# A four-layer graph network: the third layer's per-destination sums as running sums along partitions, with transfers issued from SyncE

## The chip, the cores and the metric

The kernel runs on one core of one Trainium2 chip. The metric is the device time of one execution in microseconds, the median of several runs; lower is better. PE is the matrix engine, DVE is VectorE, ACT is ScalarE, POOL is GpSimd, SP is SyncE.

## What is computed

A graph of 6250 nodes with 64 features and 200000 edges, sorted by destination, goes through four layers, each `x = x + layer(relu(layernorm(x)))`. The first is an attention over edges, the second four rounds of neighbour sums, the fourth two hops of a normalised neighbour sum. The third is the one changed:

```
features = H[src]
Y = relu(concatenate([features, Xe], axis=1) @ M_W.T + M_b)
Z = segment_sum(Y, dst, num_segments=6250)
H_next = relu(concatenate([H, Z], axis=1) @ U_W.T + U_b)
```

`Xe` is 200000 x 64, so each edge has a message of 64 numbers, and `Z` sums the messages of the edges with the same destination.

## The kernel before

Nodes are padded to 49 tiles of 128 (6272), edges to 1568 chunks of 128 (200704). The stages run one after the other, with a barrier between them: attention loop over the edges and its combination (first layer, which also counts a dense matrix A of edge counts), second layer on A with matrix products, then `last_layers`: a table `H @ M_h.T + b` written to DRAM (`tab_l`), the edge loop `sum_chunks` (L1003), the update `update_pieces` (L1206), and the two hops of the fourth layer on the transposed matrix AT.

`sum_chunks` works on groups of 8 chunks, 196 in all; four groups make a block, of which there are 49, and two groups a half block. The loop is written once and repeated by hardware loops; `steps` gives its order to every engine. The order on each engine is the order of the code:

- POOL gathers the rows of `tab_l` for the sources of a group, 8 indirect DMAs of 128 rows (L1193), once the index list `ixs` is there and the buffer `gl` has been read.
- PE multiplies the edge features `ea` by the weights (L1100), then transposes half a row block of A (49 products with the identity per block, L1110), which has nothing to do with the messages and is done here for the fourth layer, then does the sums (L1118). An fp32 product shows as two matmul records.
- DVE compares, for a whole group, the destinations of the chunk's 128 edges along the free dimension (`dall`, a list broadcast to all partitions) with the destination of the edge in each partition (`dst`), which gives `S` (128 x 8 x 128, L1082); then it adds the product and the gathered rows (`t1`, L1088).
- ACT evicts the transposes (L1148), stores the block of AT, does the ReLU (`msg`, L1160), issues the loads of index list, destination list and features for the group two half blocks later (L1135, L1137, L1140), and evicts and stores the sums (L1169, L1171).

In this layout an edge's number within its chunk is its partition. `S` times `msg` gives, in the row of every edge, the sum over all edges of its chunk with the same destination. The update gathers for each node the row of its last edge (`last_row`) and adds a carry for nodes whose edges begin in an earlier chunk: the last rows of the 1568 chunks are loaded, transposed in 14 pieces, summed by a scan of 1568 columns, transposed back and scattered to DRAM by 14 indirect DMAs (L1466), and the carry rows `U` are loaded again (L1258) and multiplied by a mask (L1335). After this, 7 pieces of 7 node tiles are summed (L1340, L1342), multiplied by the weights, normalised and split for the hops.

Of the kernel before, what the change touches and what calls it, by code (L numbers as in the profile page):

```python
# [293 lines left out]
def carry_rows(nc, g, step, dump, node, a, b):  # L294
# [4 lines left out]
    e = [g.next_c[:, k, :] for k in range(4)]  # L299
# [11 lines left out]
    step(v.tensor_copy(g.carry_to[:, :], node[:, :]))  # L311
# [70 lines left out]
def segment_ends(nc, g, top):  # L382

    g.last_row = top.sb("last_row", [P, NT], I32)
    g.last_f = top.sb("last_f", [P, NT])
    g.has = top.sb("has", [P, NT])
# [5 lines left out]
    with Stage(nc, "ends") as st:  # L392
# [86 lines left out]
        with st.block() as block:  # L479
# [6 lines left out]
            def _(dve):  # L486
# [14 lines left out]
                step(v.tensor_tensor(g.con[:, :], tmp[:, :], g.has[:, :], ALU.mult))  # L501
                step(v.tensor_tensor(tmp[:, :], cl[:, :], z[:, :], ALU.subtract))
# [11 lines left out]
                carry_rows(nc, g, step, dump, node, ca, cb)  # L514
# [488 lines left out]
def sum_chunks(nc, g, name, wb):  # L1003
# [3 lines left out]
    with Stage(nc, name) as st:  # L1007
# [4 lines left out]
        halves = (range(0, (NK + 1) // 2), range((NK + 1) // 2, NK))  # L1012
        dst_i = st.sb("dst_i", [P, NCH], I32)
        dst = st.sb("dst", [P, NCH])
# [3 lines left out]
        dall = [st.sb(f"dall{s}", [P, G, P], I32) for s in range(RB)]  # L1018
        ea = [st.sb(f"ea{s}", [D, G * P]) for s in range(RB)]
        S = [st.sb(f"S{s}", [P, G, P]) for s in range(RB)]  # L1020
# [3 lines left out]
        o = [st.sb(f"o{s}", [P, G, D]) for s in range(RB)]  # L1024
        a = [st.sb(f"a{s}", [P, NP], BF16) for s in range(R)]
        at = [st.sb(f"at{s}", [P, NT, P], BF16) for s in range(R)]
        pb = [st.ps(f"pb{s}", [P, G, D]) for s in range(R)]
        pm = [st.ps(f"pm{s}", [P, G, D]) for s in range(R)]
        pt = [st.ps(f"pt{k}", [P, 512]) for k in range(TB)]
        s_c, s_k, s_one, s_go, s_tp, s_tv = (st.sem(k) for k in ("c", "k", "one", "go", "tp", "tv"))  # L1030
        s_msg, s_mm, s_ev, s_a, s_st, s_mb, s_t1 = (
            [st.sem(f"{k}{s}") for s in range(R)] for k in ("msg", "mm", "ev", "a", "st", "mb", "t1"))
        s_da, s_S, s_out, s_ea, s_ix = ([st.sem(f"{k}{s}") for s in range(RB)] for k in ("da", "S", "out", "ea", "ix"))
# [4 lines left out]

        def wait_earlier(eng, sem, u):

            if not (isinstance(u, int) and u < 2):
                eng.wait_ge(sem, u - 1)
        Arows = g.A[0:NP * HI, :].rearrange("(n h) l -> n (h l)", h=HI)
        with st.block() as block:

            @block.sync
            def _(sp):
                sp.dma_start(dst_i[:, :], g.d["dst_cols"]).then_inc(s_c, 16)
                sp.dma_start(wbs[:, :], wb).then_inc(s_c, 16)
                sp.wait_ge(s_c, 32)  # L1050
                sp.sem_inc(s_k, 1)

            @block.vector
            def _(dve):
                nc.vector.tensor_copy(eye[:, :], g.ident[:, :]).then_inc(s_one, 1)
                dve.wait_ge(s_k, 1)
                nc.vector.tensor_copy(dst[:, :], dst_i[:, :]).then_inc(s_one, 1)
# [14 lines left out]
        with st.block() as block:  # L1072

            @block.vector
            def _(dve):
                def body(u, dt, b, n, h):
                    for s in range(R):
                        c0 = u * (R * G) + s * G
                        q = h * R + s
                        wait_earlier(dve, s_mm[s], u)  # L1080
                        dve.wait_ge(s_da[q], dt * 16 + 16)
# [4 lines left out]
                        dve.wait_ge(s_mb[s], u + 1)  # L1086
                        dve.wait_ge(s_gl[q], dt * (16 * G) + 16 * G)
                        nc.vector.tensor_tensor(t1[q][:, :, :], pb[s][:, :, :], gl[q][:, :, :], ALU.add)\  # L1088
                            .then_inc(s_t1[s], 1)

                steps(dve, body)

            @block.tensor
            def _(pe):
                def body(u, dt, b, n, h):
                    for s in range(R):
                        wait_reuse(pe, s_t1[s], u)
                        pe.wait_ge(s_ea[h * R + s], dt * 16 + 16)
                        for j in range(G):
                            mm = nc.tensor.matmul(pb[s][:, j, :], ea[h * R + s][:, j * P:(j + 1) * P], wbs[:, :],  # L1100
                                                  start=True, stop=True)
                        mm.then_inc(s_mb[s], 1)
                    if h == 0:
                        pe.wait_ge(s_a[b], n * 16 + 16)
                    for k in halves[h]:
                        before = k - TB if k >= TB else max(j for j in range(NK) if j % TB == k % TB) - NK
                        if before >= 0 or not (isinstance(dt, int) and dt == 0):
                            pe.wait_ge(s_tv, dt * NK + (before + 1))
                        for m, q in enumerate(blocks[k]):
                            mm = nc.tensor.matmul(pt[k % TB][:, m * P:(m + 1) * P], a[b][:, q * P:(q + 1) * P],  # L1110
                                                  eye[:, :], start=True, stop=True)
                        mm.then_inc(s_tp, 1)
                    for s in range(R):
                        wait_reuse(pe, s_ev[s], u)
                        pe.wait_ge(s_S[h * R + s], dt + 1)
                        pe.wait_ge(s_msg[s], u + 1)
# [3 lines left out]
                        mm.then_inc(s_mm[s], 1)  # L1120
# [4 lines left out]
            def _(act):  # L1125
                def load_block(dt, b):
                    if not known(dt, 2):
                        act.wait_ge(s_tp, dt * NK + (-NK))
                    act.dma_start(a[b][:, :], Arows[bass.ds(dt * P, P), :]).then_inc(s_a[b], 16)

                def load_group(u, dt, h, s):
                    c0 = u * (R * G) + s * G
                    q = h * R + s
                    wait_reuse(act, s_gl[q], dt * (16 * G))
                    act.dma_start(ixs[q][:, :], g.d["src_cols"][:, bass.ds(c0, G)]).then_inc(s_ix[q], 16)  # L1135
                    wait_reuse(act, s_S[q], dt)
                    act.dma_start(dall[q][:, :, :].rearrange("p g e -> p (g e)"),  # L1137
                                  g.d["dst"][bass.ds(c0 * P, G * P)].partition_broadcast(P)).then_inc(s_da[q], 16)
                    wait_earlier(act, s_mb[s], u)
                    act.dma_start(ea[q][:, :], g.d["ea64T"][:, bass.ds(c0 * P, G * P)]).then_inc(s_ea[q], 16)  # L1140

                def body(u, dt, b, n, h):
                    if h == 0:
                        wait_reuse(act, s_st[b], n * 16)
# [1154 lines left out]
```

## Time and profile before

| | us |
|---|---|
| timed runs, median of 3 | 6479.86 (6473.62 to 6487.33) |
| profiled execution, span from first to last instruction | 8670.1 |
| attention loop | 448.6 to 4102 |
| second layer and table | 4102 to 5105.9 |
| set-up and loop of `sum_chunks` | 5105.9 to 8087.5 |
| `update_pieces` | 8087.5 to 8255.8 |
| two hops | 8255.8 to 8670.1 |

The profiled execution is 2190 us longer than the timed runs; no other time of it is given. A row of a timeline has the start, the duration, the engine, the line of the kernel, the operation with its output and inputs, and in brackets the idle time before it with what ended it. A releaser called "issue" means that the engine waited for nothing that the profile shows. For a gather, the duration is GpSimd's work of issuing it, and not the landing of the data.

### The profile page before, as it was taken

The numbers are of one execution on the slowest core, as the hardware profiler recorded it, in microseconds if no ns is written. First come the engines' busy times: TensorE is split into PE (matmuls) and PEld (weight loads), VectorE is DVE, ScalarE is ACT, GpSimd is POOL, SyncE is SP. The second block draws the span as 40 slices with busy tenths as digits, with TensorE's granted clock in tenths as the row PEclk, the third lists the DMA queues.
The fourth block names the chain that finished last, engine by engine and source line by source line (L and its number), as shares of the span: only waits on it lengthen the run. The fifth ranks groups of instructions, "written<-read, shape, count | busy, mean of one in ns | idle before, by whom it ended". The sixth has DMA issues, their size and how long they took to land. (4 is left out here: it accounts for less than half of the span.)

```text
span 8670.1 us, 115438 instructions
## 1 busy us (share of the span) xinstructions
PE 5309.3 (61%) x35178; PEld 4390.0 (51%) x35178; DVE 2969.1 (34%) x3937; ACT 1847.1 (21%) x3914; POOL 3549.7 (41%) x3427
## 2 busy tenths in 40 slices
PE   2256556566666556667199955555565555656599
PEld 2234344444444434445089955555455554545499
DVE  6545544555544554445532121111111111111321
ACT  0023333333333333334000001112111111211200
POOL 5554353344444334344300025454554545555400
PEclk9567776776766776667589965555555555555599
DMA  8133333333333333333289934444444444444298
GB/s 304 38 96 97 105 98 91 97 107 95 110 95 94 96 102 95 92 96 105 65 288 365 365 117 138 144 131 152 124 150 140 136 146 129 153 132 144 78 375 337
DMA packets 659238, 1262.19 MB, mean 146 GB/s; under 512 B 167977, under 2 KB 467562, under 8 KB 633364
## 3 DMA queue, kind: packets, MB, share of 16 engines
q10 hardware_dynamic: 254028, 651.47, 23.4%
q1 hardware_dynamic: 295624, 491.69, 15.8%
q0 software_dynamic: 109184, 115.05, 6.1%
q14 instruction: 319, 2.61, 0.1%
q8 instruction: 83, 1.36, 0.1%
HBM read 924.66 MB, written 490.51 MB: 163 GB/s over the span
## 5 line engine op out<-in xcount | busy, mean ns | idle before, releaser
L697 POOL DMA_INDIRECT att_gl<-tab_l,att_ix x1568 | 1617.2, 1031 | 2013.0 <-DVE att_msg L850 1468.4
L1193 POOL DMA_INDIRECT sum_gl<-tab_l,sum_ixs x1568 | 1552.8, 990 | 1445.2 <-DMA sum_ixs<-in_src_cols 920.4
L938 ACT ACTIVATE att_acc<-att_pc 128x392 bf16<-128x392 f32 x2352 | 1085.4, 496 | 2271.2 <-remote 1131.8
L716 PE MATMUL att_pc<-att_acc,att_ohv 128*128 128x392 bf16 x2352 | 901.0, 383 | 989.7 <-ACT att_acc L938 523.4
L1088 DVE TENSOR_TENSOR sum_t<-sum_pb,sum_gl 128x512 f32<-128x512 f32 x196 | 135.3, 690 | 2596.8 <-remote 1890.2
L713 PE MATMUL att_pc<-att_ohl,att_ohv 128*128 128x392 bf16 x2352 | 904.0, 384 | 145.0 <-DVE att_ohl L813 84.5
L716 PEld LDWEIGHTS att_pc<-att_acc,att_ohv 128*128 128x128 bf16 x2352 | 248.2, 106 | 1435.5 <-ACT att_acc L938 787.1
L1110 PE MATMUL sum_pt<-sum_eye,sum_a 128*128 128x128 bf16 x2401 | 361.5, 301 | 869.6 <-issue 786.9
L1118 PE MATMUL sum_pm<-sum_msg,sum_S 128*128 128x64 f32 x3136 | 651.5, 403 | 260.6 <-ACT sum_msg L1160 258.7
L1100 PE MATMUL sum_pb<-sum_wbs,sum_ea 64*128 64x64 f32 x3136 | 704.7, 415 | 149.8 <-issue 122.3
L754 PE MATMUL att_pm<-att_msg,att_S 128*128 128x69 f32 x3136 | 618.4, 357 | 289.8 <-issue 145.2
L1118 PEld LDWEIGHTS sum_pm<-sum_msg,sum_S 128*128 128x128 f32 x3136 | 633.3, 313 | 282.1 <-ACT sum_msg L1160 230.6
L1100 PEld LDWEIGHTS sum_pb<-sum_wbs,sum_ea 64*128 64x128 f32 x3136 | 684.0, 327 | 149.5 <-issue 110.6
L1110 PEld LDWEIGHTS sum_pt<-sum_eye,sum_a 128*128 128x128 bf16 x2401 | 242.8, 136 | 994.3 <-issue 870.2
L732 PEld LDWEIGHTS att_pl<-att_xe,att_S 128*128 128x128 f32 x3136 | 643.8, 231 | 162.5 <-issue 142.7
L754 PEld LDWEIGHTS att_pm<-att_msg,att_S 128*128 128x128 f32 x3136 | 572.5, 271 | 299.5 <-issue 294.7
L1148 ACT ACTIVATE sum_at<-sum_pt 128x512 bf16<-128x512 f32 (+1 forms) x637 | 307.4, 591 | 1544.3 <-remote 672.4
L801 DVE TENSOR_TENSOR att_S<-att_dall,att_dst 128x896 f32<-128x896 int32 x224 | 245.0, 1094 | 1109.6 <-remote 926.3
L1932 PE MATMUL l_pn<-l_E,l_a 128*128 128x192 bf16 x7203 | 603.2, 246 | 12.0 <-DVE l_E L1803 12.0
L1932 PEld LDWEIGHTS l_pn<-l_E,l_a 128*128 128x128 bf16 x7203 | 595.5, 98 | 14.1 <-issue 12.2
L732 PE MATMUL att_pl<-att_xe,att_S 128*128 128x64 f32 x3136 | 582.0, 288 | 0.0
L813 DVE TENSOR_TENSOR att_ohl<-att_c_lo,cnt_lo 128x2352 bf16<-128x2352 f16 x448 | 547.3, 1222 | 0.0
(373 smaller groups left out, 5241.2 us busy)
## 6 DMA issues: line engine op xcount, KB each, us to landing
A<-att_acc SPq DMA_DIRECT2D x2352, 98.0 KB
l_a<-A SPq DMA_DIRECT2D x147, 1568.0 KB, 9.1
att_dall<-in_dst ACTq DMA_DIRECT2D x224, 448.0 KB
sum_dall<-in_dst ACTq DMA_DIRECT2D x196, 512.0 KB
hop_at<-AT SPq DMA_DIRECT2D x56, 1568.0 KB, 8.8
sum_a<-A ACTq DMA_DIRECT2D x49, 1568.0 KB, 9.5
AT<-sum_at ACTq DMA_DIRECT2D x49, 1568.0 KB, 6.3
l_at<-AT SPq DMA_DIRECT2D x42, 1568.0 KB, 8.8
```

Source lines behind the costliest of these rows:

```text
L697: nc.gpsimd.indirect_dma_start(out=gl[s][:, c, :], out_offset=None, in_=g.tab_l, in_offset=bass.IndirectOffsetOnAxis(ap=ix[s][:, c:c + 1], ...
L713: nc.tensor.matmul(pc[c][m % 2][:, 0:LO], ohv[c][h][:, m, :, 0], ohl[c][h][:, m // 2, :, m % 2], start=True, stop=False)
L716: nc.tensor.matmul(pc[c][m % 2][:, 0:LO], ohv[c][h][:, m, :, 1], acc[c][(at0[t] + m - 1) % CR][:, :], start=False, stop=True).then_inc(s_m ...
L732: mm = nc.tensor.matmul(pl[k % 2][:, j * D:(j + 1) * D], S[t // NQ][:, k * GQ + j, :], xe[k][:, j, :], start=False, stop=j == GQ - 1, skip ...
L754: mm = nc.tensor.matmul(pm[:, j * W0:(j + 1) * W0], S[s][:, q * GQ + j, :], msg[:, q * GQ + j, :], start=True, stop=True)
L813: v.tensor_tensor(ohl[c][h][:, 0:w // 2, :, :], spread(c_lo2[:, :, :].unsqueeze(1), [P, w // 2, LO, 2]), spread(g.lo[:, bass.ds(n0, w)].re ...
L938: nc.scalar.activation(acc[c][n % CR][:, :], pc[c][m % 2][:, 0:LO], ACT.Copy).then_inc(s_acc[c], 1)
L1100: mm = nc.tensor.matmul(pb[s][:, j, :], ea[h * R + s][:, j * P:(j + 1) * P], wbs[:, :], start=True, stop=True)
L1110: mm = nc.tensor.matmul(pt[k % TB][:, m * P:(m + 1) * P], a[b][:, q * P:(q + 1) * P], eye[:, :], start=True, stop=True)
L1118: mm = nc.tensor.matmul(pm[s][:, j, :], S[h * R + s][:, j, :], msg[h * R + s][:, j, :], start=True, stop=True)
L1193: nc.gpsimd.indirect_dma_start(out=gl[q][:, j, :], out_offset=None, in_=g.tab_l, in_offset=bass.IndirectOffsetOnAxis(ap=ixs[q][:, j:j + 1] ...
L1932: mm = nc.tensor.matmul(pn[k][q // 2][:, q % 2 * 3 * D:(q % 2 + 1) * 3 * D], a[c][:, t, q * P:(q + 1) * P], E3[p % 2][:, c * PIECE + t, :] ...
```

## The change

Edges are laid out along partitions: partition p has the edges p x 1568 to p x 1568 + 1567, and chunk c is column c of all of them. Consecutive edges of one destination then lie in the same partition in consecutive chunks, and the sum within a destination is a running sum from chunk to chunk: `run[c] = run[c-1] * same[c] + msg[c]`, where `same` says whether an edge has the destination of the one before. This takes one scalar_tensor_tensor per chunk on DVE, each waiting for the one before by a semaphore, and delayed by one group against the add. The comparison `S`, the destination lists, the sums on PE, their evictions and the buffers for them go. PE's transposes are dealt out in quarters behind the products of the four groups, and the products have four PSUM buffers (two before). All loads and stores of the loop are issued by SP, which has nothing to issue there before. Carries are now between 128 partitions and not between 1568 chunks: one transpose each way, a scan of 128 columns, one scatter, and no mask.

```diff
-        dst = st.sb("dst", [P, NCH])
+        same = st.sb("same", [P, NCH])
...
+                v.tensor_tensor(same[:, 1:NCH], dst_i[:, 1:NCH], dst_i[:, 0:NCH - 1], ALU.is_equal).then_inc(s_one, 1)
+                step(v.tensor_copy(next_f[:, :, 0], next_i[:, :]))
+                dve.wait_ge(s_io, 1)
+                step(v.tensor_copy(dump[:, :], dump_i[:, :]))
+                carry_rows(nc, g, step, [next_f[:, k, :] for k in range(4)], dump, node, ca, cb, g.carry_p)
...
+                def add(dt, q):
+                    wait_reuse(dve, s_msg[q], dt)
+                    dve.wait_ge(s_mb[q], dt + 1)
+                    dve.wait_ge(s_gl[q], dt * (16 * G) + 16 * G)
+                    v.tensor_tensor(t1[q][:, :, :], pb[q][:, :, :], gl[q][:, :, :], ALU.add).then_inc(s_t1[q], 1)
+
+                def sums(dt, q):
+                    c0 = dt * (RB * G) + q * G
+                    wait_reuse(dve, s_out[q], dt * 16)
+                    dve.wait_ge(s_msg[q], dt + 1)
+                    for j in range(G):
+                        before = run[q][:, j - 1, :] if j else run[(q - 1) % RB][:, G - 1, :]
+                        if not known(c0 + j, 1):
+                            dve.wait_ge(s_run, c0 + j)
+                        v.scalar_tensor_tensor(out=run[q][:, j, :], in0=before, scalar=same[:, bass.ds(c0 + j, 1)],
+                                               in1=msg[q][:, j, :], op0=ALU.mult, op1=ALU.add).then_inc(s_run, 1)
...
-                        nc.vector.tensor_tensor(
-                            S[q][:, :, :], dall[q][:, :, :],
-                            spread(dst[:, bass.ds(c0, G)].unsqueeze(2), [P, G, P]), ALU.is_equal)\
-                            .then_inc(s_S[q], 1)
...
-                        for j in range(G):
-                            mm = nc.tensor.matmul(pm[s][:, j, :], S[h * R + s][:, j, :], msg[h * R + s][:, j, :],
-                                                  start=True, stop=True)
...
+                def load_group(dt, q):
+                    c0 = dt * (RB * G) + q * G
+                    wait_reuse(sp, s_gl[q], dt * (16 * G))
+                    sp.dma_start(ixs[q][:, :], g.d["src_rows_p"][:, bass.ds(c0, G)]).then_inc(s_ix[q], 16)
+                    wait_reuse(sp, s_mb[q], dt)
+                    sp.dma_start(ea[q][:, :], g.d["ea64P"][:, bass.ds(c0 * P, G * P)]).then_inc(s_ea[q], 16)
+
+                def keep(dt, q):
+                    sp.wait_ge(s_run, dt * (RB * G) + (q * G + G))
+                    sp.dma_start(tot_rows(g, dt * (RB * G) + q * G), run[q][:, :, :]).then_inc(s_out[q], 16)
...
+                        if not (isinstance(dt, int) and dt + 1 >= NT):
+                            load_group(dt + 1, q)
+                        if q:
+                            keep(dt, q - 1)
+                        elif not known(dt, 1):
+                            keep(dt - 1, RB - 1)
...
-                step(vec.tensor_tensor(U[:, :, :], U[:, :, :], spread(g.con[:, :].unsqueeze(2), [P, NT, W]), ALU.mult))
...
-                for b in range(B):
-                    nc.gpsimd.indirect_dma_start(
-                        out=carries, in_=crow[:, b, :], in_offset=None,
-                        out_offset=bass.IndirectOffsetOnAxis(ap=g.carry_to[:, b:b + 1], axis=0)).then_inc(s_sc, 16)
+                nc.gpsimd.indirect_dma_start(
+                    out=carries, in_=crow[:, :], in_offset=None,
+                    out_offset=bass.IndirectOffsetOnAxis(ap=g.carry_p[:, 0:1], axis=0)).then_inc(s_sc, 16)
```

VectorE in the body of the loop, before: a comparison and an add per group (two groups shown; ISA and REGISTER_ALU are waits and sums on registers).

```order
L1081 ISA
L1082 ISA
L1082 TENSOR_TENSOR sum_S<-sum_dall,sum_dst 128x1024
L1086 REGISTER_ALU
L1087 ISA
L1088 TENSOR_TENSOR sum_t<-sum_pb,sum_gl 128x512
L1082 ISA
L1082 TENSOR_TENSOR sum_S<-sum_dall,sum_dst 128x1024
L1088 TENSOR_TENSOR sum_t<-sum_pb,sum_gl 128x512
```

The same place after the change: the end of one chain, the add, and the beginning of the next chain.

```order
L1108 SCALAR_TENSOR_TENSOR sum_run<-sum_run,sum_same,sum_msg 128x64
L1098 TENSOR_TENSOR sum_t<-sum_pb,sum_gl 128x512
L86 REGISTER_ALU
L1107 REGISTER_ALU
L1108 ISA
L1108 SCALAR_TENSOR_TENSOR sum_run<-sum_run,sum_same,sum_msg 128x64
L1107 REGISTER_ALU
L1108 ISA
L1108 SCALAR_TENSOR_TENSOR sum_run<-sum_run,sum_same,sum_msg 128x64
```

The comparison is gone, and eight dependent steps, each with a register sum and a register wait in front, follow each add.

GpSimd in the update stage, before (`upd_J` are the rows of the nodes' last edges, `car` the carries in DRAM):

```order
L1458 DMA upd_J<-tot,top_last_row 128x64 x14
L1466 DMA car<-upd_crow,top_carry_to 7840x64 x14
L1458 DMA upd_J<-tot,top_last_row 128x64 x35
```

and after:

```order
L1476 DMA upd_J<-tot,top_last_edge 128x64 x14
L1483 DMA car<-upd_crow,top_carry_p 7840x64
L1476 DMA upd_J<-tot,top_last_edge 128x64 x35
```

Thirteen of the 14 scatters between the gathers are gone.

## Rows read from the trace of the kernel before

**Rows 1.** The page of the profile, its span.
```profile
span 8670.1 us, 115438 instructions
```

**Rows 2.** Stretches: length, busy us (records) by engine, granted clock, DMA share, GB/s.
```profile
core 0: us, PE busy (x) PEld busy (x) DVE busy (x) ACT busy (x) POOL busy (x), PEclk, DMA share, GB/s
...
448.60:4102.00 3653.40, 2264.13 (x11515) 1541.46 (x11515) 1857.90 (x2511) 1253.08 (x2791) 1617.15 (x1568) 0.70 0.34 99
...
5119.30:8067.60 2948.30, 1694.55 (x8612) 1549.11 (x8612) 352.47 (x389) 536.53 (x1019) 1552.76 (x1568) 0.51 0.46 139
8067.60:8087.50 19.90, 11.47 (x63) 10.93 (x62) 2.52 (x3) 5.08 (x11) 0.00 (x0) 0.50 0.42 112
8087.50:8255.80 168.30, 75.49 (x322) 63.44 (x322) 61.00 (x124) 35.07 (x72) 65.70 (x63) 0.50 0.21 58
```

**Rows 3.** The page's groups: out<-in, count | busy us, mean ns | idle before, releaser.
```profile
L697 POOL DMA_INDIRECT att_gl<-tab_l,att_ix x1568 | 1617.2, 1031 | 2013.0 <-DVE att_msg L850 1468.4
L1193 POOL DMA_INDIRECT sum_gl<-tab_l,sum_ixs x1568 | 1552.8, 990 | 1445.2 <-DMA sum_ixs<-in_src_cols 920.4
```

**Rows 4.** Gathers of both loops: count, ns min/median/max, first and last start; a wait.
```profile
L697 POOL DMA_INDIRECT att_gl<-tab_l,att_ix x1568: 939/945/1870, 448.6 to 4068.3; - x196
...
L1193 POOL DMA_INDIRECT sum_gl<-tab_l,sum_ixs x1568: 938/945/1962, 5119.3 to 8066.6; - x196
...
  DMA sum_ixs<-in_src_cols: 920.4, 58
```

**Rows 5.** Timeline of PE, quick stretch: start us, us, line, what, count.
```profile
6533.61 7.09 PE L1100 MATMUL sum_pb<-sum_wbs,sum_ea 64*128 64x64 f32 x32
...
6545.37 5.75 PE L1118 MATMUL sum_pm<-sum_msg,sum_S 128*128 128x64 f32 x32 [1.67 <-ACT sum_msg L1160]
6551.05 1.33 PE L1100 MATMUL sum_pb<-sum_wbs,sum_ea 64*128 64x64 f32 x5
```

**Rows 6.** The same columns as in the stretches: a slow and a quick one.
```profile
6499.80:6517.00 17.20, 2.55 (x10) 1.40 (x9) 0.00 (x0) 0.60 (x1) 13.18 (x14) 0.50 0.16 42
6533.60:6551.10 17.50, 15.83 (x94) 15.41 (x93) 3.65 (x4) 5.87 (x11) 11.89 (x11) 0.60 0.78 227
```

**Rows 7.** Timeline: gathers beside VectorE's add and comparison in the changed loop.
```profile
6537.17 0.94 POOL L1193 DMA_INDIRECT sum_gl<-tab_l,sum_ixs  x1 [0.30 <-issue]
6537.42 0.69 DVE L1088 TENSOR_TENSOR sum_t<-sum_pb,sum_gl 128x512 f32<-128x512 f32 x1 [12.13 <-PE sum_pb L1100]
6538.03 1.22 DVE L1082 TENSOR_TENSOR sum_S<-sum_dall,sum_dst 128x1024 f32<-128x1024 int32 x1
6538.42 1.65 POOL L1193 DMA_INDIRECT sum_gl<-tab_l,sum_ixs  x1 [0.30 <-issue]
```

**Rows 8.** Timeline of the update stage, GpSimd, SyncE and VectorE.
```profile
8088.16 0.94 POOL L1458 DMA_INDIRECT upd_J<-tot,top_last_row  x1 [20.62 <-POOLq L101]
...
8108.34 0.95 POOL L1466 DMA_INDIRECT car<-upd_crow,top_carry_to  x1 [0.30 <-issue]
...
8126.71 0.77 SPq L1258 DMA_DIRECT2D l_y<-car  x1
...
8137.83 3.42 DVE L1335 TENSOR_TENSOR l_y<-l_y,top_con 128x3136 f32<-128x3136 f32 x1 [30.30 <-DMA l_y<-car]
8138.24 3.83 POOL L1458 DMA_INDIRECT upd_J<-tot,top_last_row  x1 [0.30 <-issue]
8141.29 0.62 DVE L1340 TENSOR_TENSOR upd_J<-upd_J,top_has 128x448 f32<-128x448 f32 x1
```

**Rows 9.** Timeline of the end of the changed loop.
```profile
8072.38 0.69 DVE L1088 TENSOR_TENSOR sum_t<-sum_pb,sum_gl 128x512 f32<-128x512 f32 x1 [1.10 <-DMA sum_gl<-tab_l,sum_ixs]
...
8081.99 0.34 ACTq L1171 DMA_DIRECT2D tot<-sum_o  x1
```

**Rows 10.** Groups of VectorE by shape, 5119 to 8255 us: count | busy us, mean ns.
```profile
L1352 DVE SCALAR_TENSOR_TENSOR upd_xm<-upd_mean,top_x 128x448 f32<-128x448 f32 x7 | 4.4, 624 | 0.2
...
L1360 DVE TENSOR_TENSOR upd_v<-upd_v,upd_deg 128x7 f32<-128x7 f32 x7 | 1.2, 166 | 0.2
```

More of the change, by code:

```diff
@@ L291, in node_table, with carry_rows @@
             after(nc, g, st, res)
-def carry_rows(nc, g, step, dump, node, a, b):
+def carry_rows(nc, g, step, e, dump, node, a, b, to):
     v = nc.vector
-    e = [g.next_c[:, k, :] for k in range(4)]
     step(v.tensor_copy(node[:, :], e[0]))
@@ L310, in carry_rows @@
     step(v.tensor_tensor(node[:, :], node[:, :], dump[:, :], ALU.add))
-    step(v.tensor_copy(g.carry_to[:, :], node[:, :]))
+    step(v.tensor_copy(to[:, :], node[:, :]))
 class Degrees:
@@ L501, in _ @@
                 step(v.tensor_tensor(g.con[:, :], tmp[:, :], g.has[:, :], ALU.mult))
+                step(v.scalar_tensor_tensor(out=tmp[:, :], in0=cl[:, :], scalar=float(P), in1=cnt[:, :],
+                                            op0=ALU.mult, op1=ALU.add))
+                step(v.tensor_scalar(tmp[:, :], tmp[:, :], -1.0, 0.0, ALU.add, ALU.max))
+                step(v.tensor_scalar(tmp[:, :], tmp[:, :], float(EP - 1), None, ALU.min))
+                step(v.tensor_copy(g.last_edge[:, :], tmp[:, :]))
                 step(v.tensor_tensor(tmp[:, :], cl[:, :], z[:, :], ALU.subtract))
@@ L513, in _ @@
                 step(v.tensor_copy(dump[:, :], dump_i[:, :]))
-                carry_rows(nc, g, step, dump, node, ca, cb)
+                carry_rows(nc, g, step, [g.next_c[:, k, :] for k in range(4)], dump, node, ca, cb, g.carry_to)
 def expand_rows(nc, g, st, res):
@@ L1101, in body @@
                                                   start=True, stop=True)
[L1102 to L1116, printed above, removed]
[L1117 to L1120 removed]
+                        mm.then_inc(s_mb[q], 1)
@@ new lines, in body @@
+                        if q == 0:
+                            pe.wait_ge(s_a[b], n * 16 + 16)
+                        for k in quarters[q]:
+                            before = k - TB if k >= TB else max(j for j in range(NK) if j % TB == k % TB) - NK
+                            if before >= 0 or not known(dt, 1):
+                                pe.wait_ge(s_tv, dt * NK + (before + 1))
+                            for m, r in enumerate(blocks[k]):
+                                mm = nc.tensor.matmul(pt[k % TB][:, m * P:(m + 1) * P], a[b][:, r * P:(r + 1) * P],
+                                                      eye[:, :], start=True, stop=True)
+                            mm.then_inc(s_tp, 1)
@@ L1125, in _, with body @@
             def _(act):
+                def body(u, dt, b, n, h):
+                    for s in range(R):
+                        q = h * R + s
+                        if q == 0:
+                            wait_reuse(act, s_st[b], n * 16)
+                        for k in quarters[q]:
+                            r = blocks[k]
+                            act.wait_ge(s_tp, dt * NK + (k + 1))
+                            nc.scalar.activation(at[b][:, r[0]:r[-1] + 1, :],
+                                                 pt[k % TB][:, 0:len(r) * P].rearrange("p (m e) -> p m e", e=P), ACT.Copy)\
+                                .then_inc(s_tv, 1)
+                        if not known(dt, 1):
+                            act.wait_ge(s_run, dt * (RB * G) + (q * G + G - RB * G))
+                        act.wait_ge(s_t1[q], dt + 1)
+                        nc.scalar.activation(msg[q][:, :, :], t1[q][:, :, :], ACT.Relu).then_inc(s_msg[q], 1)
@@ L1126, in load_block, with _ @@
+                steps(act, body)
+            @block.sync
+            def _(sp):
                 def load_block(dt, b):
                     if not known(dt, 2):
[L1128 to L1140, printed above, removed]
@@ L1142, in body @@
[L1142 to L1150 removed]
+                        sp.wait_ge(s_tp, dt * NK + (-NK))
@@ L2251, in lay_out @@
     a["dst_next"] = nxt.reshape(4, CQ, CP).transpose(2, 0, 1)
+    a["src_rows_p"] = src.reshape(P, NCH)
+    a["dst_rows_p"] = dst.reshape(P, NCH)
+    a["last_p"] = dst[NCH - 1::NCH]
+    a["last_p_prev"] = np.concatenate([np.full(1, -1, np.int32), dst[NCH - 1::NCH][:-1]])
+    beyond = np.concatenate([dst, np.full(2 * NCH, NP, np.int32)])
+    a["next_p"] = np.stack([beyond[np.arange(1, P + 1) * NCH + k] for k in (-1, 0, NCH - 1, NCH)], 1)
     rows = np.full((NCH + 1, P + 2), NP + 1, np.int32)
```

161 lines of the change are left out of this document (72 added, 89 removed).

## The prediction

> **What bounds the kernel now.** I read the stages first, then the engine that sets the pace of the changed one. The profiled execution spans 8670.1 us, the timed runs have a median of 6479.9: 2190.2 us less, so before anything is summed it must be settled which waits of the trace are not in the time. The change touches the edge loop of the third layer (2948.3 us of the span) and the two short stages behind it; the attention loop of the first layer takes 3653.4 [rows 1, 2].
>
> Both loops issue 1568 indirect gathers on GpSimd. One lasts 945 ns in the median, and undisturbed ones follow each other every 1.25 us [rows 3, 4, 7]. That is a floor of 1568 x 1.25 = 1960 us for each loop, whatever the other engines do. In the third layer's loop the 2948 us are this floor, plus 1552.8 - 1568 x 0.945 = 71 us by which gathers last longer, plus some 917 us in which GpSimd waits; the view of the gathers names 920.4 us in 58 waits, for the index load [rows 3, 4]. ScalarE issues that load behind its ReLU, in order behind its evictions of PE's transposes, so the wait goes back to PE.
>
> And PE has two speeds there that the work doesn't explain. In one stretch of 17.2 us it leaves 10 matmul records and is busy 2.55 us; in another of 17.5 it leaves 94, at about the same granted clock (0.50, 0.60) [rows 6]. In the quick stretch a whole half block (two groups' products, 28 transposes, two groups' sums) goes from 6533.61 to 6551.05, 17.4 us, with 16 gathers (20.0 us) to be fed by it [rows 5]. At that speed PE never holds GpSimd up; only the slow stretch does, once in each of the 49 blocks. The time says that much of this is not in the timed runs: the attention loop has its own floor of 1960 of 3619.7 us between its first and last gather [rows 4], so it can give back 1660 at most, and the changed loop must give at least 530 of the 2190. Timed, it lasts between 1960 and 2418 us. I take the case in which GpSimd's waits are gone there. Then GpSimd is active all the time and not for 2031 of 2948 us, and the 71 us of long gathers grow to 71 x 2948 / 2031 = 103. **Timed loop before: 2063 us.**
>
> **Part by part.** *The comparison and the sums on PE go.* 196 comparisons (1.22 us on VectorE), the loads that feed them, 1568 fp32 products and 196 evictions go. With GpSimd as the bound, none of this counts on PE or ScalarE. What counts is what the comparison does to a gather: the one that begins at 6538.42, 0.39 us into a comparison, takes 1.65 us, while one beside the add, which has an operand in PSUM, takes 0.94 [rows 7]. So all 103 us are put down to comparisons (0.53 us each), and go. This is where a page speaks otherwise. The Trainium skill ("SBUF — State Buffer", section "Who interferes with whom") says that a tensor_tensor with two SBUF inputs takes only the shared read interface, which descriptor generation is inferred not to need. By that rule neither comparison nor new sum would lengthen a gather, and this term would be 0. The trace disagrees with 1.65 against 0.94 us, and I go by the trace.
>
> *1568 running sums come.* Each is a scalar_tensor_tensor over 128x64 with two SBUF inputs, the same kind that holds a gather up, only shorter. Nearest rows: 166 ns for 7 elements, 624 ns for 448 [rows 10], so 1.04 ns an element and 0.225 us for 64. Eight in each 10 us of gathers are 18% of the time. A gather that meets one waits for what is left of it, 0.11 us on average: 1568 x 0.18 x 0.11 = 32 us. Lower bound 0, upper bound under the rivals. That VectorE lets a gather through between two of its instructions, I read from 8138.24: this gather ends at 8142.07, 0.82 us after the end of L1335 (8141.25), although L1340 began 0.04 us later [rows 8]. **Loop: 1960 + 32 = 1992, 71 us less.**
>
> *The chain on VectorE* doesn't bind. A step waits for the one before, and has a register instruction and a register wait in front: 0.225 us plus at least the 0.04 between two instructions in rows 8, at a guess 0.35. With the add of 0.69 a group needs 3.5 of its 10 us. It would bind from (10 - 0.7) / 8 = 1.16 us a step.
>
> *SyncE issues.* Per group now index load, feature load, store; per block a write of the transposed block and a load. In front of each index load it waits for the store before, which waits for the running sums. Behind that wait are queued the next index and feature loads. The index load for group q of the next block is issued when the gather of group q has landed, three groups (30 us) before GpSimd needs it, and a running sum is 3 us late at most, so nobody waits. ScalarE loses its issue work and 196 evictions: nothing, it isn't the bound. The destination lists (196 x 128x1024 int32, 100 MB) that no longer move were beside the gathers: 0, or a gain in landing, which no one waits for but at the end.
>
> *Beginning and end of the loop.* The set-up gets a comparison over 1567 columns in place of a cast, 13 dependent tiny operations and 4 more in an earlier stage: 17 x 0.17 [rows 10] and their waits, +5 us, in the open. At the end 9.6 us pass from the last add to the last store (8072.38 to 8081.99) [rows 9], through ReLU, product and eviction; now add 0.7, ReLU, and two groups of 8 steps, 6.4: -3 us.
>
> *Update stage.* 14 scatters of carries become one. The first piece's sums begin at 8141.29, behind the multiplication of the carry rows (8137.83, 3.42 us) and their load, issued at 8126.71, after the 14 scatters from 8108.34 on. Now: 14 gathers from 8088.16 at 1.25 us, one scatter at about 8106, its landing, load issued near 8108, the same 11.1 us to land, no multiplication: near 8119 [rows 8]. -22 us. The pieces behind are a chain over PE, ScalarE and VectorE that keeps its spacing, and the row gathers (35 x 1.25 = 44 us from 8107 on) stay ahead of it, so all of the 22 should reach the end. The two hops behind it start earlier by that and stay as they are.
>
> **Sum:** -71 + 5 - 3 - 22 = -91. Against the median: 6479.9 - 91 = **6389 us**. The span of the profiled execution falls by more, as the 917 us of waits hang on PE, which loses a third of the block's work and the step between add and index load: 8670 - 91 - up to 917, so down to 7660.
>
> **Rivals.**
> *PE's slow stretches are partly in the timed runs.* Then the timed loop before lasts up to 2418, and the change takes away up to 426 instead of 71: between 6389 and 6034. For: rows 6 show nothing that PE waits for, so they can't exclude a real cause. Against: the attention loop has 1524 us of waits of its own, enough for most of the 2190. Shared in proportion, with the longer gathers counted, 46 us would be left in this loop: 6343.
> *The long gathers don't change*, because they aren't in the time or the short operations cost as much as the long ones: only +5 - 3 - 22 is left, 6460. In this case the gathers would lie where the page of the Trainium skill named above puts them.
> *Slower: a gather can't get in between chained sums.* If it has to wait for the end of a chain of 8 (2.8 us), one gather in each group waits some 2.2 us: 196 x 2.2 = 431 instead of 103, so 6479.9 + 328 - 20 = 6788. It decides from 0.63 us a group ((103 + 20) / 196). Against it stands 8138.24 in rows 8; for it, that this is one case, with a 3.4 us operation.
> *Slower: a step of the chain takes over 1.16 us.* At 1.4 a group takes 11.9 us and the loop 2333: 6730. Against: the gaps of 0.04 in rows 8; for: register waits between the steps, which no row shows.
>
> **How the numbers follow.** Forecast (6330 to 6445) 0.55; PE rival 0.15; no change of long gathers 0.15; blocked by the chain 0.10; slow steps 0.05. The two slower cases, 0.15, lie above; of the PE rival I leave out what is below 6200, about 0.05. Range 6200 to 6480. A measurement of this kernel can tell about 0.2% (13 us) from no change. The no-change case lies 20 us below the median and falls on either side of that line, half each. Faster 0.55 + 0.15 + 0.08 = 0.78; same 0.07; slower 0.15.
>
> **What would show it.** In the trace after: gathers of the loop at 1.25 us with few above 1.1 us, and their busy sum near 1482 + 32 = 1514 instead of 1552.8; running sums of 0.2 to 0.25 us, under 4 us a chain; first piece's sums some 32 us after the update stage begins, not 54; GpSimd's waits for the index load far below 920. Wrong if the busy sum of the gathers rises, if GpSimd waits for the add, or if the median moves by much more than the loop's floor allows.

## The result

The changed kernel takes 6384.8 us (median; 6383.0 to 6396.1), the kernel before 6479.5: ratio 0.9857, 95% interval 0.9843 to 0.9871. The forecast was 6389. Its profiled execution spans 6384.6 us, so this trace is a trace of the timed kernel, which that of before (8670.1, [rows 1]) was not. A second profile of the unchanged kernel before came out at 6476.3 us; the comparison below uses that one in place of [rows 1 to 4]. Two timed executions, one of the kernel before (13610.9 us) and one of the run with twice the products (6945.5), had a lower mean granted clock (0.303 and 0.599, against some 0.73 in the others) and are left out of all ratios.

First the page of the changed kernel, its span and the group of the gathers:

```profile
span 6384.6 us, 112327 instructions
...
L1221 POOL DMA_INDIRECT sum_gl<-tab_l,sum_ixs x1568 | 1483.9, 946 | 495.5 <-issue 477.7
```

Then the views of the gathers and of the running sums (count: ns min/median/max, first and last start):

```profile
L1221 POOL DMA_INDIRECT sum_gl<-tab_l,sum_ixs x1568: 942/947/1007, 3866.9 to 5827.5; - x196
...
L1108 DVE SCALAR_TENSOR_TENSOR sum_run<-sum_run,sum_same,sum_msg x1568: 274/283/350, 3888.8 to 5835.6; 128x64 f32<-128x64 f32 x196
```

The loop lasts 1960.6 us from first to last gather, which is the floor of 1568 x 1.25. No gather takes longer than 1.007 us (before: up to 1.962, [rows 4]), GpSimd waits for nothing but itself ("issue" is the 0.30 us between gathers), and the 1568 running sums cost at most 2 us of gathers (1483.9 against 1568 x 0.945). One group of them on the timeline:

```profile
4805.26 0.95 POOL L1221 DMA_INDIRECT sum_gl<-tab_l,sum_ixs  x1 [0.30 <-issue]
4805.26 3.20 DVE L1108 SCALAR_TENSOR_TENSOR sum_run<-sum_run,sum_same,sum_msg 128x64 f32<-128x64 f32 x8
...
4806.51 0.95 POOL L1221 DMA_INDIRECT sum_gl<-tab_l,sum_ixs  x1 [0.30 <-issue]
...
4807.76 0.94 POOL L1221 DMA_INDIRECT sum_gl<-tab_l,sum_ixs  x1 [0.30 <-issue]
```

Three gathers begin inside the chain of eight and keep their 0.95 us. The chain takes 3.20 us, about 0.4 a step.

The loop as a stretch of the changed kernel (columns as in [rows 2]):

```profile
3866.80:5828.50 1961.70, 1010.67 (x5537) 907.24 (x5537) 558.76 (x1747) 417.72 (x832) 1483.88 (x1568) 0.50 0.49 157
```

PE is at 52% busy in the loop, at a granted clock of 0.50 (1.2 GHz), and DVE at 28%.

### The profile page after: what moved, and what is told of

Its sections match the earlier page's. It is cut to its first block and busy times, and to the rows that moved or that the text cites. A ratio compares the mean times of both kernels' runs of the same rounds, so it can differ in the third digit from the quotient of the medians.

```text
span 6384.6 us, 112327 instructions
## 1 busy us (share of the span) xinstructions
PE 4411.9 (69%) x32016; PEld 3631.9 (57%) x32016; DVE 3174.4 (50%) x5301; ACT 1726.3 (27%) x3718; POOL 3776.5 (59%) x3415
## 5 line engine op out<-in xcount | busy, mean ns | idle before, releaser
L703 POOL DMA_INDIRECT att_gl<-tab_l,att_ix x1568 | 1930.2, 1231 | 487.4 <-issue 470.5
L1221 POOL DMA_INDIRECT sum_gl<-tab_l,sum_ixs x1568 | 1483.9, 946 | 495.5 <-issue 477.7
L1141 PE MATMUL sum_pt<-sum_eye,sum_a 128*128 128x128 bf16 x2401 | 309.7, 310 | 932.2 <-ACT sum_at L1157 892.7
L722 PE MATMUL att_pc<-att_acc,att_ohv 128*128 128x392 bf16 x2352 | 863.0, 367 | 114.2 <-ACT att_acc L944 110.4
L738 PEld LDWEIGHTS att_pl<-att_xe,att_S 128*128 128x128 f32 x3136 | 605.1, 218 | 162.4 <-issue 140.8
L760 PE MATMUL att_pm<-att_msg,att_S 128*128 128x69 f32 x3136 | 560.0, 333 | 4.6 <-ACT att_o L933 2.7
L1163 ACT ACTIVATE sum_msg<-sum_t 128x512 f32<-128x512 f32 x196 | 123.7, 631 | 1541.6 <-DVE sum_t L1098 1463.9
L1108 DVE SCALAR_TENSOR_TENSOR sum_run<-sum_run,sum_same,sum_msg 128x64 f32<-128x64 f32 x1568 | 444.7, 284 | 172.4 <-DVE sum_run L1108 5.5
L760 PEld LDWEIGHTS att_pm<-att_msg,att_S 128*128 128x128 f32 x3136 | 518.7, 248 | 9.3 <-ACT att_o L933 3.5
L719 PEld LDWEIGHTS att_pc<-att_ohl,att_ohv 128*128 128x128 bf16 x2352 | 312.9, 133 | 368.4 <-DVE att_ohl L819 303.6
```

What stands on the lines that cost most here:

```text
L703: nc.gpsimd.indirect_dma_start(out=gl[s][:, c, :], out_offset=None, in_=g.tab_l, in_offset=bass.IndirectOffsetOnAxis(ap=ix[s][:, c:c + 1], ...
L719: nc.tensor.matmul(pc[c][m % 2][:, 0:LO], ohv[c][h][:, m, :, 0], ohl[c][h][:, m // 2, :, m % 2], start=True, stop=False)
L722: nc.tensor.matmul(pc[c][m % 2][:, 0:LO], ohv[c][h][:, m, :, 1], acc[c][(at0[t] + m - 1) % CR][:, :], start=False, stop=True).then_inc(s_m ...
L738: mm = nc.tensor.matmul(pl[k % 2][:, j * D:(j + 1) * D], S[t // NQ][:, k * GQ + j, :], xe[k][:, j, :], start=False, stop=j == GQ - 1, skip ...
L760: mm = nc.tensor.matmul(pm[:, j * W0:(j + 1) * W0], S[s][:, q * GQ + j, :], msg[:, q * GQ + j, :], start=True, stop=True)
L1108: v.scalar_tensor_tensor(out=run[q][:, j, :], in0=before, scalar=same[:, bass.ds(c0 + j, 1)], in1=msg[q][:, j, :], op0=ALU.mult, op1=ALU.a ...
```

## The experiments

All ratios are to the kernel before, measured on the same chip.

### The kernel before, once more

No edit. 

> The kernel before, unchanged, for a second profile. Theory (GpSimd sets the pace of the third layer's edge loop, comparisons lengthen its gathers, PE's slow stretches are not in the time): 6480 us; if this profile spans about 6480, its loop takes 2050 to 2070 us from first to last gather, the gathers' busy sum is near 1482 + 100 = 1585 us, and GpSimd's waits for the index load are near zero. Rival (PE's slow stretches are partly in the time): the same time, but the busy sum stays near 1553 and some 50 us or more of waits for the index load are left.

6473.9 us (ratio 1.000, 0.999 to 1.001). The span, and the group of the gathers in the view of GpSimd's groups, which also names the wait for the index load:

```profile
span 6476.3 us, 115438 instructions
...
L1193 POOL DMA_INDIRECT sum_gl<-tab_l,sum_ixs x1568 | 1556.4, 993 | 524.7 <-issue 477.2 <-DMA sum_ixs<-in_src_cols 47.4
```

and the view of the gathers:

```profile
L1193 POOL DMA_INDIRECT sum_gl<-tab_l,sum_ixs x1568: 941/947/1996, 3857.0 to 5890.3; - x196
```

The 920 us of waits for the index load in [rows 4] are gone; of the 47.4 left, none lies inside the loop (no two of its gathers start more than 2.3 us apart). The loop lasts 2033.3 us: 1959 of pitches and 74 by which gathers are longer (1556.4 - 1568 x 0.945), where 100 were expected. PE's slow stretches are neither in this execution nor, by their times near 6475 us, in the timed ones that are compared.

The same trace shows how a comparison holds a gather up:

```profile
4909.42 0.95 POOL L1193 DMA_INDIRECT sum_gl<-tab_l,sum_ixs  x1 [0.30 <-issue]
4910.02 1.22 DVE L1082 TENSOR_TENSOR sum_S<-sum_dall,sum_dst 128x1024 f32<-128x1024 int32 x1
4910.67 1.39 POOL L1193 DMA_INDIRECT sum_gl<-tab_l,sum_ixs  x1 [0.31 <-issue]
```

The gather of 4909.42 has begun 0.60 us before the comparison and isn't touched. The one of 4910.67 ends at 4912.06, 0.82 us after the comparison's end (4911.24). 167 of the 1568 gathers last longer than 1 us, on average 0.44 us more than the 0.945 of an undisturbed one.

Counted over the whole loop, this is a rule. 182 gathers begin inside a comparison that has more than 0.125 us left. All those for which the comparison had begun at least 0.04 us earlier end 0.81 to 0.83 us after it (the few with hardly more than 0.125 us left show no difference); the three that begin within 0.03 us of its start aren't touched. Since 0.945 - 0.82 is 0.125, a held gather waits for what the comparison has left beyond 0.125 us. All of the 74 us are in such gathers (73.3).

### A comparison put back into the changed kernel

```diff
                 def add(dt, q):
...
+                    v.tensor_tensor(junk[:, :, :], dst_i[:, 0:G * P].rearrange("p (g e) -> p g e", e=P),
+                                    spread(same[:, 0:G].unsqueeze(2), [P, G, P]), ALU.is_equal).then_inc(s_junk, 1)
                     v.tensor_tensor(t1[q][:, :, :], pb[q][:, :, :], gl[q][:, :, :], ALU.add).then_inc(s_t1[q], 1)
```

> The changed kernel with one comparison per group put back on VectorE, of the same size (128x1024, two operands in SBUF), whose output nobody reads. Theory (such an instruction holds up the gather that meets it): 196 x 0.53 to 0.6 us, 104 to 118 us more than 6385, so 6489 to 6503, gathers' busy sum near 1590. Rival (a comparison doesn't delay gathers, the gain came from elsewhere): 6385 to 6387.

6422.6 us (0.9898 to 0.9931): 38 us more than the changed kernel and than the next one, measured beside it, about a third of what was expected, and outside the rival too. The view of the gathers:

```profile
L1226 POOL DMA_INDIRECT sum_gl<-tab_l,sum_ixs x1568: 942/947/1977, 3867.5 to 5860.0; - x196
```

and the timeline around one comparison:

```profile
4805.36 0.94 POOL L1226 DMA_INDIRECT sum_gl<-tab_l,sum_ixs  x1 [0.30 <-issue]
4805.51 1.23 DVE L1101 TENSOR_TENSOR sum_junk<-sum_dst_i,sum_same 128x1024 f32<-128x1024 int32 x1 [5.07 <-DMA sum_gl<-tab_l,sum_ixs]
4806.61 0.95 POOL L1226 DMA_INDIRECT sum_gl<-tab_l,sum_ixs  x1 [0.30 <-issue]
```

Here the comparison begins 0.15 us behind a gather's start and ends 0.13 behind the next one's, and neither is longer. In this kernel it follows the landing of a gather directly, and most comparisons fall in this place (125 of 196 begin within 0.2 us behind a gather's start); 104 gathers begin inside a comparison with more than 0.125 us left, where before it were 182, and only 66 last over 1 us (167 before). An operation of 1.2 us can fit between two gathers, so its cost depends on where in the 1.25 us it begins, and 196 of them cost between 32 us (the loop is 1992.5 long) and the 74 of before. My expectation had taken 0.53 us each from the first trace.

### The same comparison with one operand from PSUM

```diff
-                                    spread(same[:, 0:G].unsqueeze(2), [P, G, P]), ALU.is_equal).then_inc(s_junk, 1)
+                                    spread(pb[q][:, :, 0:1], [P, G, P]), ALU.is_equal).then_inc(s_junk, 1)
```

> As the one before, but the comparison's second operand comes from PSUM: same number of elements, same place, output read by nobody. Theory (it is the second operand in SBUF that holds a gather up, not the load on VectorE): 6385 to 6387, busy sum 1484. Rival (any long instruction on VectorE, or its delay of the add, costs): as much as with both in SBUF, about 6490.

6384.5 us (0.9846 to 0.9879), the changed kernel's time. The page's groups of the gathers and of the added comparison:

```profile
L1226 POOL DMA_INDIRECT sum_gl<-tab_l,sum_ixs x1568 | 1481.1, 945 | 495.3 <-issue 477.6
...
L1101 DVE TENSOR_TENSOR sum_junk<-sum_dst_i,sum_pb 128x1024 f32<-128x1024 int32 x196 | 239.4, 1221 | 1023.3 <-DMA sum_gl<-tab_l,sum_ixs 1022.9
```

196 operations of 1221 ns, as long as the comparisons, and not a microsecond of gathers. 138 gathers begin inside one with more than 0.125 us left, and none is held. It is the second SBUF operand that holds them up; neither the length alone nor the later add does. The Trainium skill ("SBUF — State Buffer", "Who interferes with whom") says that a VectorE instruction with at most one SBUF input, outside the 2-port modes, doesn't contend with GpSimd: with that, this trace agrees. That tensor_tensor with two SBUF inputs leaves descriptor generation alone, which the same section infers, does not hold for these gathers. They take their index list from SBUF, and by the section's own rule that an instruction with two SBUF inputs contends with a GpSimd instruction that reads SBUF, they could be held; the prediction left that rule out.

### The kernel before with a narrow comparison

```diff
-                            S[q][:, :, :], dall[q][:, :, :],
-                            spread(dst[:, bass.ds(c0, G)].unsqueeze(2), [P, G, P]), ALU.is_equal)\
+                            S[q][:, :, 0:8], dall[q][:, :, 0:8],
+                            spread(dst[:, bass.ds(c0, G)].unsqueeze(2), [P, G, 8]), ALU.is_equal)\
```

> The kernel before with the comparison 8 columns wide in place of 128, so that most of S stays zero and the sums are left out; all loads, products and evictions stay. Theory: the held-up gathers go, 103 us less, about 6377, with all of PE's work still there. Rival (PE's work of the sums is what the change saved): 6480, no change.

6401.8 us (0.9867 to 0.9900): 70 us less than before, where 103 were expected. The view of the gathers:

```profile
L1195 POOL DMA_INDIRECT sum_gl<-tab_l,sum_ixs x1568: 940/944/990, 3861.8 to 5818.0; - x196
```

All of PE's products for the sums, their evictions and the loads of the destination lists are still there, and no gather is longer than 0.990 us. The loop lasts 1956.2 us, 77 less than before, and begins 5 us later. So the comparison's width alone carries the loop's whole gain, and neither PE's share of the work (1619 us busy in this loop, 1625 before) nor the 100 MB of lists carries any of it.

### Twice the products on PE

```diff
-                        for j in range(G):
+                        for j in [*range(G), *range(G)]:
                             mm = nc.tensor.matmul(pb[q][:, j, :], ea[q][:, j * P:(j + 1) * P], wbs[:, :],
```

> The changed kernel with every product of edge features and weights done twice into the same place: 1568 fp32 products more on PE, some 14 us in each block of 40, as much as the sums that the change takes from PE. Theory (GpSimd's 1.25 us per gather is the pace, PE hides behind it): the time of the changed kernel, ratio to before 0.985 to 0.987. Rival (PE's work counts): up to 49 x 14 us more, anything from 0.99 up.

6383.9 us (0.9839 to 0.9876), no change. With as much on PE as before the change (1665.9 us busy in the loop, 1625.0 before), the loop is at its floor: gathers from 3862.5 to 5823.7 us, 1961.2. The rival of PE falls.

### The update stage's part alone

```diff
-                for b in range(B):
+                for b in range(1):
                     nc.gpsimd.indirect_dma_start(
                         out=carries, in_=crow[:, b, :], in_offset=None,
...
-                step(vec.tensor_tensor(U[:, :, :], U[:, :, :], spread(g.con[:, :].unsqueeze(2), [P, NT, W]), ALU.mult))
```

> The kernel before with 1 scatter of carries in place of 14 and without the mask on the carry rows (so most carries and the mask are left out); loop and transposes as they were. Theory: 13 x 1.24 + 3.4 = 19.6 us less, of the 22 that the first piece's sums begin earlier in the changed kernel; ratio 0.9970. Rival (the pieces behind wait for something else and the gain of the stage's beginning is lost): 0.9985 to 1.

6455.2 us, ratio 0.9978 (0.9968 to 0.9988): 8 to 21 us less, with the expected 20 at the edge; the time alone would hardly tell it from the rival. The traces do: the stage begins at 5905.4 and its first sums at 5939.7, 34.3 us; in the second profile of before 5910.2 and 5964.0, 53.7. That is 19.4 us, and from there to the first product of the hops it is 99.0 us and 98.9, so nothing of it is lost there.

### Transfers issued from ScalarE

```diff
                         nc.scalar.activation(msg[q][:, :, :], t1[q][:, :, :], ACT.Relu).then_inc(s_msg[q], 1)
+                        if not (isinstance(dt, int) and dt + 1 >= NT):
+                            load_group(dt + 1, q)
+                        if q:
+                            keep(dt, q - 1)
+                        elif not known(dt, 1):
+                            keep(dt - 1, RB - 1)
```

> The changed kernel with all transfers of the loop issued from ScalarE in place of SyncE, behind each group's ReLU. Theory (the issuing queue is worth nothing, since index loads are three groups early): ratio to before 0.985 to 0.987. Rival (ScalarE's evictions wait behind the wait for the running sums, and with them PE's transposes and the index load): slower than the changed kernel by 1% or more.

6379.5 us (0.9843 to 0.9877). The queue that issues is worth nothing here, as costed.

### A second chain

```diff
+                        v.scalar_tensor_tensor(out=junk[q][:, j, :], in0=t1[q][:, j, :], scalar=0.5,
+                                               in1=t1[q][:, j, :], op0=ALU.mult, op1=ALU.add).then_inc(s_junk, 1)
```

> The changed kernel with a second scalar_tensor_tensor of 128x64, both operands in SBUF, behind each running sum (output read by nobody): 1568 more. Theory, after the trace of the changed kernel (such a short operation hardly delays a gather: 2 us for 1568 of them): up to 10 us more, ratio 0.9857 to 0.9872. Rival, the term as it stood in the prediction (each delays the gathers for its whole duration): 32 us more or above, 0.9907 and up.

6384.7 us (0.9844 to 0.9876), no change. The view of the gathers:

```profile
L1227 POOL DMA_INDIRECT sum_gl<-tab_l,sum_ixs x1568: 940/944/1025, 3867.9 to 5828.3; - x196
```

3136 short operations with two SBUF operands, and the longest gather is 1.025 us. The term of 32 us in the sum was wrong in kind, not in size only.

It isn't the kind of instruction that spares them. The attention loop of the changed kernel has a scalar_tensor_tensor of 0.63 us that reads a tile in SBUF as both operands, and it holds gathers by the same 0.82 us behind its end (1330.46 and 1331.27 here):

```profile
1329.83 0.63 DVE L830 SCALAR_TENSOR_TENSOR att_t<-att_t 128x448 f32<-128x448 f32 x1
1329.95 1.32 POOL L703 DMA_INDIRECT att_gl<-tab_l,att_ix  x1 [0.30 <-issue]
```

It does so to 56 of the 68 gathers that begin inside it with more than 0.125 us left; the other 12 begin within 0.05 us of its start. A running sum obeys the same rule and is nearly too short for it. In the changed kernel 155 gathers begin inside one with more than 0.125 us left. Those that begin less than 0.09 us behind its start aren't held, and of its 0.283 us only some 0.07 are then left in which a gather can be: 19 gathers are lengthened by more than 0.01 us, none by more than 0.062, and all of them together by 0.6 us.

### The same hold in a loop that the change leaves alone

```diff
-                    v.tensor_tensor(S[s][:, k * GQ:(k + 1) * GQ, :], dall[k][:, :, :],
+                    v.tensor_tensor(S[s][:, k * GQ:(k + 1) * GQ, 0:8], dall[k][:, :, 0:8],
```

> The changed kernel with the comparison of the first layer's attention loop 8 columns wide in place of 128 (most of its S stays zero, so the attention's sums are left out). It asks whether the same hold exists in a loop that the change doesn't touch. Theory: 224 comparisons of 1.09 us with two operands in SBUF cost 0.2 to 0.45 us of gathers each, 45 to 100 us less than 6385: 6285 to 6340. Rival (that loop is set by PE or VectorE): 6380 and above.

6263.2 us, ratio 0.9669 (0.9652 to 0.9686): by the two ratios 122 us less than the changed kernel, more than the 100 expected. The attention loop's gathers have 1930.2 us of busy time in the changed kernel and 1806.9 here, 123 less, and from first to last they take 2407.1 and 2283.6 us, also 123 less:

```profile
L704 POOL DMA_INDIRECT att_gl<-tab_l,att_ix x1568 | 1806.9, 1152 | 487.3 <-issue 471.9
```

That loop too is paced by GpSimd, and 448 us of its 2407 (1930.2 - 1568 x 0.945) are held-up gathers in the changed kernel.

### Cutting long operations: a faster version

```diff
-                    v.tensor_tensor(ohl[c][h][:, 0:w // 2, :, :], spread(c_lo2[:, :, :].unsqueeze(1), [P, w // 2, LO, 2]),
...
+                    for half in range(2):
+                        lo, n = half * (LO // 2), LO // 2
+                        one = v.tensor_tensor(
+                            ohl[c][h][:, 0:w // 2, lo:lo + n, :], spread(c_lo2[:, lo:lo + n, :].unsqueeze(1), [P, w // 2, n, 2]),
...
+                    one.then_inc(s_oh[c], 1)
```

> The changed kernel with the longest VectorE operation of the attention loop (128x2352, 1.38 us, two operands in SBUF, 280 times; and 168 of 128x1568) cut into two halves of the same kind. Theory (a gather waits for what is left of the operation it meets, so the cost goes with the square of its length): up to 85 + 25 us less for gathers, against 448 more fixed costs on VectorE (some 50 us, not on the path as long as it is not the bound): 6300 to 6350. Rival (VectorE, 77% busy, becomes the bound, or gathers meet the second half instead): 6385 or slower.

6269.9 us, ratio 0.9680 (0.9663 to 0.9697): by the two ratios 115 us less than the changed kernel, with the full computation. The page's group of the attention loop's gathers and, from the groups of VectorE by shape, the operation that was cut, in the changed kernel:

```profile
L703 POOL DMA_INDIRECT att_gl<-tab_l,att_ix x1568 | 1930.2, 1231 | 487.4 <-issue 470.5
```

```profile
L819 DVE TENSOR_TENSOR att_ohl<-att_c_lo,cnt_lo 128x2352 bf16<-128x2352 f16 x280 | 385.6, 1377 | 0.0
```

The same two views of this kernel:

```profile
L703 POOL DMA_INDIRECT att_gl<-tab_l,att_ix x1568 | 1754.5, 1119 | 530.0 <-issue 473.5
```

```profile
L821 DVE TENSOR_TENSOR att_ohl<-att_c_lo,cnt_lo 128x1176 bf16<-128x1176 f16 x560 | 404.3, 763 | 0.0
```

1377 ns become twice 763, VectorE does more, and the gathers' busy time falls by 176 us. Of that 133 reach the loop (2407.1 us from first to last gather before, 2274.0 now); the rest became waits, and the third layer's loop begins 120 us earlier (3746.7, 3866.9), so 13 more are lost between the two loops, which was not followed up. Cutting the comparison too:

> As the one before, with the attention loop's comparison (128x896, 1.09 us, 224 times) cut in two as well. Theory: another 20 to 40 us less than with the first cut alone. Rival: no less than with the first cut, since VectorE gets fuller.

6294.0 us, ratio 0.9707 (0.9687 to 0.9727): slower than with the first cut alone by 24 us, as the rival said. The gathers' busy time falls by another 36 us (1718.2), but GpSimd waits more (588.5 us idle, 530.0 with one cut), and the loop lasts 2295.8. Which wait comes in was not followed up.

## Why the prediction was right, point by point

**The bound.** Right: GpSimd's gathers pace the loop, at 1.25 us each, and PE hides (twice the products; the narrow comparison). So was the reading of the long profile by means of the floors: the waits for the index load, 920 us [rows 3, 4], were not in the timed kernel.

**The held-up gathers of before, 103 us.** Oversized by 29: the second profile has 74, and the narrow comparison gives 70 in time. The step that failed is the scaling of 71 us by the share of the time in which GpSimd was active. In the first trace 100 gathers are longer than 1 us, with 0.72 us more than 0.945 on average, in the second 167, with 0.44: more of them are met, as the scaling assumed, but for less, since the comparison falls elsewhere in the 1.25 us, and the sum hardly moves. How much that matters, the comparison put back into the changed kernel shows with 32. The loop took 2033 us, not 2063.

**The running sums, 32 us.** Measured: at most 2, and 0.6 by the gathers that the trace shows lengthened. The operation lasts 0.283 us, longer than the 0.225 worked out, so the error isn't there, but in "a gather that meets one waits for what is left of it". It waits only for what is left beyond 0.125 us, and only if the operation has been under way for a while when the gather begins (about 0.04 us with the comparison, 0.09 with a running sum). For an operation of 1.2 us that takes little away, for one of 0.283 nearly all. The same count for the second chain has no gather above 1.025 us. The loop took 1961 us, not 1992.

**A reading that shows less than it says.** The gather "beside the add" in [rows 7] began at 6537.17, 0.25 us before the add, and a gather that has begun isn't held by an operation of either kind. That an operand in PSUM spares the gathers rests on the comparison with one operand from PSUM, and on the adds of the changed kernel: 43 gathers begin inside one with more than 0.125 us left, and none is held.

**The difference,** 71 us, measured 72.7 (2033.3 - 1960.6): right, because both terms were about 30 too large and stand with opposite signs. The forecast's closeness owes that much to luck.

**Set-up, end, update stage.** +5: the first gather starts 13.6 us after the set-up's first transfer in before (3843.4 to 3857.0) and 17.9 in after (3848.9 to 3866.9), +4.3. -3 at the end: from last gather to the update's first transfer 19.9 us and 15.8, -4.1. -22: first sums 53.7 and 31.7 us after the stage's start, as forecast to a few tenths. In after:

```profile
5861.50 1.00 POOL L1483 DMA_INDIRECT car<-upd_crow,top_carry_p  x1 [0.30 <-issue]
...
5863.83 0.77 SPq L1285 DMA_DIRECT2D l_y<-car  x1
...
5874.98 0.63 DVE L1358 TENSOR_TENSOR upd_J<-upd_J,top_has 128x448 f32<-128x448 f32 x1 [25.67 <-DMA l_y<-car]
```

The load is issued 2.3 us behind the one scatter, and the sums begin 11.2 us later; in [rows 8] 18.4 us pass from first scatter to load. From the first sums to the hops' first product it is 99.1 us here and 98.9 in the second profile of before, so all of the 22 us arrive. The parts give 4.3 - 72.7 - 4.1 - 22.1 = -94.6, the medians -94.7, the two profiles -91.7; in these the attention loop, which the change leaves alone, is 4.2 us longer after it (2407.1, 2402.9).

**SyncE, the chain.** Right: no cost (transfers from ScalarE), and 0.4 us a step against the 1.16 from which it would bind.

**The rivals.** PE's stretches in the time: excluded by the second profile and by twice the products. No change of long gathers, and with it the inference of the Trainium skill named above ("SBUF — State Buffer", "Who interferes with whom"): excluded by the narrow comparison and by the one with an operand from PSUM. Blocked by the chain: excluded by the trace and by the second chain.

**The span.** Forecast were 7660 to 8579 for the profiled execution; it is 6384.6. Of the 2194 us between the two profiles of before, 1217 lie in the attention loop (3619.7 [rows 4], 2402.9 in the second) and 914 in the changed one (2947.3, 2033.3): almost all of it in these two loops, and none of it in the timed runs that are compared. The step that failed here is the one that left the attention loop's 1217 us in the forecast of the next profile, although the prediction itself had found that they are not in the time.

## What to carry to other kernels

Where GpSimd's indirect gathers set the pace, their number times their pitch is the floor, and what lengthens them are VectorE operations with two SBUF operands: those of 0.6 us and more did so here, one of 0.28 hardly; narrowing, cutting, or moving one operand to PSUM gave time back, taking work from PE didn't. What such an operation costs depends on where in the pitch it begins: a comparison of the same size cost 74 us in one kernel and 32 in the other. When a profiled span and the timed runs differ by a third, set the floor of each stage against it before a wait of the trace is costed, and take a second profile if one can be had. A forecast that comes out should still be checked term by term.

## What the runs showed of the hardware

- A gather undisturbed lasts 0.945 us. One that begins at least 0.05 us behind the start of a VectorE operation of 0.6 to 1.4 us with two SBUF operands, and with more than 0.125 us of it left, ends 0.81 to 0.83 us after that operation (1.39 us long in the row above). One that begins with less of it left, or within 0.02 us of its start, or before it, isn't delayed.
- So an operation of 1.2 us delays none if it begins 0.15 us behind one gather and ends 0.13 behind the start of the next.
- The same 1.22 us operation with one operand in PSUM delays none of 1568 gathers (busy sum 1481.1 us).
- 1568 or 3136 operations of 0.28 us and less with two SBUF operands delay them by at most 2 us in all, since a running sum must have begun 0.09 us before the gather. Why that is 0.09 here and 0.04 with the longer ones was not settled.
- An execution of the same kernel under the profiler spanned 8670.1 us once and 6476.3 another time. The first has stretches in which PE leaves 10 matmul records in 17.2 us, where a quick one has 94 in 17.5, at granted clocks of 0.50 and 0.60 [rows 6]. What caused them is open.
